# Which engine copies the K and V projections out of PSUM: from ScalarE to VectorE

## The chip, the cores and the metric

The kernel runs on the 8 cores of one Trainium2 chip. Each core works on its own part of the tokens with all the weights, and no core waits for another. The metric is the device time of the slowest core in microseconds (us).

## The reference

The reference is one transformer layer over x of shape (4, 2048, 2048), with a LayerNorm ahead of and behind each half:

```python
x = x + _layernorm(attn(_layernorm(x), Wq, Wk, Wv, Wo))
x = x + _layernorm(ffn(_layernorm(x), w_gate_up, w_down))
# attn: q = h @ Wq.T (16 heads), k = h @ Wk.T, v = h @ Wv.T (4 heads of 128)
#   softmax over a causal window of 1024 keys and 4 sink keys, then y @ Wo.T
# ffn: silu(h @ Wg.T) * (h @ Wu.T), then @ w_down.T; inner size 8192
```

Each core computes 1024 rows of the output. For the keys and values it needs up to 2048 token rows (`x_kv`).

## The kernel before, in words

The kernel is written in stages: (1) LayerNorm of the 2048 token rows, transposed to feature-major `h1f`, with the K and V projections in between; (2) the Q projection; (3) attention; (4) the output projection with residual and second LayerNorm; (5) the feed-forward part; (6) the last LayerNorm and the output. The change touches stage 1 alone.

Nothing schedules the work. A recorder (`Em`) takes tasks in the order in which the Python code emits them, and gives each engine its own queue in that order. It puts a semaphore wait ahead of a task where something that the task reads or overwrites is made or read on another engine (`task`, L43 to L97). So an engine that stands at a wait holds up everything behind it in its queue, whether that needs the awaited thing or not.

Stage 1 is a loop over 16 token tiles of 128 rows (L345 to L387); `idx` counts them from 0 to 15. Two buffers `xt` take turns for the tiles. For each tile the loop emits, in this order:

- the projections that have become possible. At idx 6 five V projections (`vproj`, L319 to L332), and from idx 7 on one in each tile, always for a tile whose `h1f` was made before. At idx 4, 8 and 12 also four K projections (`kproj`, L304 to L317). One projection is 16 matmuls of 512 columns into one PSUM bank, and one copy of that bank, cast to bf16, to SBUF (`kf` or `vt`). Six banks take turns (`bank512`).
- the load of the tile by a DMA from the POOL queue (L362), and (in the first tiles) the loading and casting of the weights of K and V.
- the statistics on VectorE: four BN_STATS (L275) and a BN_AGGR (L280), then on ScalarE a logarithm (L283) and an exponential (L286) that give `rstd`, and on VectorE one small operation for `nmr` (L290).
- the normalised tile `h1t` on ScalarE (L370), 16 transposes on TensorE (L378), and one copy of 2048 columns back to `h1f` on ScalarE (L385).

After the loop two more V projections and the last four K projections follow. Then the Q projection starts (L402): its weights are loaded by SP into two staging buffers `wst` and cast to bf16 `wqr` by ScalarE (L249), two casts for each of the first two heads ahead of the first matmul group.

Of the kernel before, what the change touches and what calls it, by code (L numbers as in the profile page):

```python
# [122 lines left out]
def build_nc():  # L123
# [91 lines left out]
    em = Em()  # L215
# [81 lines left out]
    def bank512():  # L297
        i = rot[0] % 6
        rot[0] += 1
        if i < 4:  # L300
            return PA[i], PAK[i]
        return PB[i - 4], PBK[i - 4]

    def kproj(m, ts):  # L304
        bk, bkk = bank512()
        fns = []
        for c in range(16):
            fns.append(lambda t, m=m, ts=ts, c=c, bk=bk: t.matmul(  # L308
                bk, wkbf.ap()[:, m * 2048 + c * 128:m * 2048 + (c + 1) * 128],
                h1f.ap()[:, c * 2048 + ts * 512:c * 2048 + (ts + 1) * 512],  # L310
                start=(c == 0), stop=(c == 15), skip_group_check=True))
        rd = [f"wk{m}"] + [f"h1_{4 * ts + i}_{g}" for i in range(4) for g in range(2)]
        em.task("tensor", fns, reads=rd, writes=[bkk])
        em.task("scalar",
                [lambda q, m=m, ts=ts, bk=bk: q.copy(
                    kf.ap()[:, m * 2048 + ts * 512:m * 2048 + (ts + 1) * 512], bk)],
                reads=[bkk], writes=[f"k_{m}_{ts}"])  # L317

    def vproj(tb):  # L319
        bk, bkk = bank512()  # L320
        fns = []
        for c in range(16):
            fns.append(lambda t, tb=tb, c=c, bk=bk: t.matmul(  # L323
                bk, h1f.ap()[:, c * 2048 + tb * 128:c * 2048 + (tb + 1) * 128],
                wvbf.ap()[:, c * 512:(c + 1) * 512],
                start=(c == 0), stop=(c == 15), skip_group_check=True))
        rd = [f"wv{c}" for c in range(16)] + [f"h1_{tb}_{g}" for g in range(2)]
        em.task("tensor", fns, reads=rd, writes=[bkk])
        em.task("scalar",
                [lambda q, tb=tb, bk=bk: q.copy(  # L330
                    vt.ap()[:, tb * 512:(tb + 1) * 512], bk)],
                reads=[bkk], writes=[f"v_{tb}"])  # L332

# [11 lines left out]
    for idx, tb in enumerate(TB_ORDER):  # L345
# [3 lines left out]
        if idx >= 6:  # L349
            while len(vback) > 1:  # L350
                vproj(vback.pop(0))
        if idx == 4:
            for m in range(4):
                kproj(m, 2)
        elif idx == 8:
            for m in range(4):
                kproj(m, 3)
        elif idx == 12:
            for m in range(4):
                kproj(m, 0)  # L360
# [28 lines left out]
    while vback:  # L389
        vproj(vback.pop(0))  # L390
# [5 lines left out]
    for me in range(16):  # L396
        r = me % 4
        for ts in range(2):
            bk, bkk = bank512()
# [541 lines left out]
```

How the kernel before makes its waits and increments, by code:

```python
    def replay(self, eng_obj, eng_name, sems):  # L108
        for waits, fns, inc in self.items[eng_name]:
            for (s, v) in waits:
                eng_obj.wait_ge(sems[s], 16 * v if s in self.streams else v)
            last = None
            for fn in fns:
                last = fn(eng_obj)
            if inc is not None and last is not None:
                last.then_inc(sems[inc[0]], inc[1])
```

## Time and profile before

| | us |
|---|---|
| median of 3 runs | 2387.99 (2293.54 to 2585.29) |
| the profiled execution | 2291.22 |
| its span, slowest core (core 7) | 2289.6 |
| spans of the 8 cores | 2283.2 to 2289.6 |
| stage 1 (start to the last K projection) | 254 |
| stage 2 (Q projection) | 113 |

The span is the time from the first to the last instruction of the slowest core; 1.6 us of the execution's time lie around it. The busy time of an engine is what the profiler records for its instructions.
### The profile page before, as it was taken

Reading aid. Unit: us, or ns where it says so; the run is one execution under the profiler, and the core shown is the slowest. Engines: PE = TensorE matmul, PEld = TensorE weight load, DVE = VectorE, ACT = ScalarE, POOL = GpSimd, SP = SyncE. Lnnn points to the kernel's source line nnn. Section 1 sums busy time; section 2 is a strip of 40 time slices with the busy share of each in tenths; the row PEclk is TensorE's granted clock in tenths of the full one; section 3 lists DMA queues with packets and bytes.
Section 4 is the critical chain, followed back from the end, with each engine's and each line's share of the span. In section 5 each row is a group of like instructions: output and inputs, shape, how many; then the busy total and the mean of one; then the engine's idle time right before and its main releaser. Section 6 shows DMA issues by size and latency. Waiting matters only on the chain.

```text
span 2289.6 us, 23911 instructions; the slowest of 8 cores (2283.2 to 2289.6 us)
## 1 busy us (share of the span) xinstructions
PE 2045.8 (89%) x9424; PEld 905.1 (40%) x9424; DVE 447.6 (20%) x592; ACT 918.9 (40%) x907; POOL 66.4 (3%) x87
## 2 busy tenths in 40 slices
PE   0776998998888886999999999999999999999983
PEld 0333443332223443444444444444444444444442
DVE  2122002543332541000121000110100110001135
ACT  4344344776663344333332333323333323333312
POOL 1100002400000000000000000000000000000000
PEclk9888999999999998999999999999999999999995
DMA  6321356501000333444553444643444634445526
GB/s 190 125 87 60 92 149 183 176 1 49 1 1 19 127 131 129 148 151 155 180 176 101 154 150 147 186 145 127 151 156 153 178 119 147 156 156 161 181 84 236
DMA packets 75566, 298.67 MB, mean 130 GB/s; under 512 B 8512, under 2 KB 8640, under 8 KB 69056
## 3 DMA queue, kind: packets, MB, share of 16 engines
q1 hardware_dynamic: 70848, 263.58, 36.8%
q0 software_dynamic: 4608, 33.56, 4.2%
q8 instruction: 77, 1.26, 0.2%
q14 instruction: 33, 0.27, 0.0%
HBM read 280.33 MB, written 16.78 MB: 130 GB/s over the span
## 4 chain that ended last, share of the span: by engine, by line
PE 84%; ACT 9%; DVE 2%; issue 2%; DMA 2%; ACTq 0%; DVEq 0%; SPq 0%; POOL 0%; POOLq 0%
PE ps_b L666 19%; PE ps_a L674 19%; PE ps_a L707 10%; PE ps_b L707 10%; ACT pt L451 5%; PE ps_a L442 5%; PE ps_a L402 3%; PE ps_a L582 3%; PE ps_b L500 2%; PE ps_b L491 2%; PE ps_a L308 2%; PE ps_a L323 2%; PE ps_b L582 2%; PE ps_b L402 2%; ACT h1t L370 1%
## 5 line engine op out<-in xcount | busy, mean ns | idle before, releaser
L249 ACT CAST wbf<-wst 128x1024 bf16<-128x1024 f32 x384 | 394.2, 1044 | 504.6 <-DMA wst<-wgu_pe 268.7
L666 PE MATMUL ps_b<-h2f,wbf 128*128 128x512 bf16 x2048 | 454.7, 380 | 4.0 <-ACT wbf L249 4.0
L674 PE MATMUL ps_a<-h2f,wbf 128*128 128x512 bf16 x2048 | 452.5, 379 | 0.0
L666 PEld LDWEIGHTS ps_b<-h2f,wbf 128*128 128x128 bf16 x2048 | 200.7, 98 | 247.6 <-issue 7.3
L674 PEld LDWEIGHTS ps_a<-h2f,wbf 128*128 128x128 bf16 x2048 | 200.6, 98 | 241.5
L686 DVE TENSOR_TENSOR a_sb<-silu_t,ps_a 128x1024 bf16<-128x1024 f32 x64 | 78.2, 1221 | 817.6 <-PE ps_a L674 741.7
L451 ACT ACTIVATE pt<-ps_a 128x2048 bf16<-128x2048 f32 x112 | 189.7, 1694 | 104.1 <-PE ps_a L442 100.3
L707 PE MATMUL ps_a<-a_sb,wbf 128*128 128x512 bf16 x1024 | 226.2, 379 | 5.9 <-DVE a_sb L686 5.9
L707 PE MATMUL ps_b<-a_sb,wbf 128*128 128x512 bf16 x1024 | 226.2, 379 | 0.0
L682 ACT ACTIVATE silu_t<-ps_b 128x1024 f32<-128x1024 f32 x64 | 65.5, 1024 | 347.1 <-PE ps_b L666 347.1
L469 DVE TENSOR_TENSOR pt<-pt,msk 128x2048 bf16<-128x2048 bf16 (+1 forms) x112 | 113.2, 1012 | 351.1 <-ACT pt L451 339.8
L707 PEld LDWEIGHTS ps_a<-a_sb,wbf 128*128 128x128 bf16 x1024 | 99.9, 98 | 127.7 <-issue 7.8
L707 PEld LDWEIGHTS ps_b<-a_sb,wbf 128*128 128x128 bf16 x1024 | 100.2, 98 | 120.8
L442 PE MATMUL ps_a<-qf,kf 128*128 128x512 bf16 x400 | 106.8, 385 | 45.3 <-ACT pt L451 44.4
L378 PE MATMUL ps_b<-i,h1t 128*128 128x128 bf16 x256 | 24.1, 269 | 100.5 <-ACT h1t L370 100.5
L491 PE MATMUL ps_b<-pt,vt 128*128 128x512 bf16 x400 | 107.2, 386 | 3.3 <-DVE yf L531 2.6
L500 PE MATMUL ps_b<-pt,ones_bf 128*1 128x512 bf16 x400 | 106.0, 383 | 0.0
L402 PE MATMUL ps_a<-h1f,wqr 128*128 128x512 bf16 x352 | 76.9, 379 | 2.7 <-ACT wqr L249 2.7
L442 PEld LDWEIGHTS ps_a<-qf,kf 128*128 128x128 bf16 x400 | 32.0, 97 | 118.2 <-issue 96.0
L582 PE MATMUL ps_a<-wo_bf,yf 128*128 128x512 bf16 x256 | 60.5, 400 | 6.3 <-ACT h2f L628 6.3
L378 PEld LDWEIGHTS ps_b<-i,h1t 128*128 128x128 bf16 x256 | 20.8, 122 | 106.6 <-issue 106.6
L582 PE MATMUL ps_b<-wo_bf,yf 128*128 128x512 bf16 x256 | 55.9, 379 | 6.3 <-ACT h2f L628 6.3
(103 smaller groups left out, 1082.5 us busy)
## 6 DMA issues: line engine op xcount, KB each, us to landing
wst<-wgu_pe SPq DMA_DIRECT2D x256, 512.0 KB, 4.2
wst<-wd_pe SPq DMA_DIRECT2D x128, 512.0 KB, 4.5
xt<-x_kv POOLq DMA_DIRECT2D x16, 1024.0 KB, 6.1
wst<-wq_pe SPq DMA_DIRECT2D x32, 512.0 KB, 4.4
wst<-wo_t SPq DMA_DIRECT2D x32, 512.0 KB, 4.4
xo<-x_kv POOLq DMA_DIRECT2D x8, 1024.0 KB, 7.1
wst<-wk_pe SPq DMA_DIRECT2D x8, 512.0 KB, 4.7
wst<-wv_t SPq DMA_DIRECT2D x16, 256.0 KB, 3.7
```

What stands on the lines that cost most here:

```text
L249: fn = [lambda g, d=dst_ap, sl=slot, n=n: g.copy(d, sl.ap()[:, 0:n])]
L402: fns.append(lambda t, r=r, ts=ts, c=c, bk=bk: t.matmul(bk, wqr[r].ap()[:, c * 128:(c + 1) * 128], h1f.ap()[:, c * 2048 + 1024 + ts * 512: ...
L442: t.matmul(dst, kf.ap()[:, kv * 2048 + kb * 128:kv * 2048 + (kb + 1) * 128], qf.ap()[:, hh * 1024 + qs * 512:hh * 1024 + (qs + 1) * 512], ...
L451: [lambda q, src=pa[:, 0:512 * ln], st0=st0, ln=ln: q.activation(pt.ap()[:, st0 * 512:(st0 + ln) * 512], src, AF.Exp, scale=SCALE)],
L469: [lambda v, a=a, b=b: v.tensor_tensor(pt.ap()[:, a * 512:(a + b) * 512], pt.ap()[:, a * 512:(a + b) * 512], msk.ap()[:, a * 512:(a + b) * ...
L491: t.matmul(yb, vt.ap()[:, kb * 512 + kv * 128:kb * 512 + (kv + 1) * 128], pt.ap()[:, s_ * 512:(s_ + 1) * 512], start=first, stop=last, ski ...
L500: t.matmul(zb[0:1, :], ones_bf.ap(), pt.ap()[:, s_ * 512:(s_ + 1) * 512], start=first, stop=last, skip_group_check=True))
L582: fns.append(lambda t, c=c, ms=ms, tb=tb, bk=banks[ms][0]: t.matmul(bk, yf.ap()[:, c * 1024 + tb * 128:c * 1024 + (tb + 1) * 128], wo_bf.a ...
L666: fns.append(lambda t, c=c, ts=ts, rg=rg: t.matmul(PB[ts], wbf[rg].ap()[:, c * 128:(c + 1) * 128], h2f.ap()[:, c * 1024 + ts * 512:c * 102 ...
L674: fns.append(lambda t, c=c, ts=ts, ru=ru: t.matmul(pa[:, ts * 512:(ts + 1) * 512], wbf[ru].ap()[:, c * 128:(c + 1) * 128], h2f.ap()[:, c * ...
L686: [lambda v, jj=jj: v.tensor_tensor(a_sb.ap()[:, jj * 1024:(jj + 1) * 1024], silu_t.ap(), pa[:, 0:1024], ALU.mult)],
L707: fns.append(lambda t, ic=ic, ts=ts, r=r, dps=dps: t.matmul(dps[ts], wbf[r].ap()[:, ic * 128:(ic + 1) * 128], a_sb.ap()[:, ic * 1024 + ts ...
```

## The change

The copy out of PSUM at the end of each K and V projection goes to VectorE instead of ScalarE. Buffers, sizes, matmuls, DMAs and the place in the code stay. These are 16 copies to `kf` and 16 to `vt`, 32 in all.

```diff
@@ kproj, L314
-        em.task("scalar",
-                [lambda q, m=m, ts=ts, bk=bk: q.copy(
+        em.task("vector",
+                [lambda v, m=m, ts=ts, bk=bk: v.tensor_copy(
                     kf.ap()[:, m * 2048 + ts * 512:m * 2048 + (ts + 1) * 512], bk)],
                 reads=[bkk], writes=[f"k_{m}_{ts}"])
@@ vproj, L329
-        em.task("scalar",
-                [lambda q, tb=tb, bk=bk: q.copy(
+        em.task("vector",
+                [lambda v, tb=tb, bk=bk: v.tensor_copy(
                     vt.ap()[:, tb * 512:(tb + 1) * 512], bk)],
                 reads=[bkk], writes=[f"v_{tb}"])
```

Since each engine keeps the order in which the code emits, the copies move from ScalarE's queue to the same point of the emission in VectorE's queue. The orders of TensorE, POOL and SP stay as they are.

VectorE's queue before, over two tiles of the middle of the loop. In all of these rows `xt_48` and `xt_49` are the two token buffers, `bn_84` and `bn_85` the statistics of the first, `bn6b` and `bn2b` those of the second.

```order
L290 TENSOR_SCALAR nmrb<-bn2b,rstdb 128x1
L275 BN_STATS bn_84<-xt_48 128x6 x4
L280 BN_AGGR bn_85<-bn_84 128x2
L290 TENSOR_SCALAR nmr<-bn_85,rstd 128x1
L275 BN_STATS bn6b<-xt_49 128x6 x4
L280 BN_AGGR bn2b<-bn6b 128x2
L290 TENSOR_SCALAR nmrb<-bn2b,rstdb 128x1
```

The same place with the change (tiles 9 and 10):

```order
L290 TENSOR_SCALAR nmr<-bn_85,rstd 128x1
L330 CAST vt<-ps_a 128x512
L275 BN_STATS bn6b<-xt_49 128x6 x4
L280 BN_AGGR bn2b<-bn6b 128x2
L290 TENSOR_SCALAR nmrb<-bn2b,rstdb 128x1
L330 CAST vt<-ps_b 128x512
L275 BN_STATS bn_84<-xt_48 128x6 x4
L280 BN_AGGR bn_85<-bn_84 128x2
L290 TENSOR_SCALAR nmr<-bn_85,rstd 128x1
```

A copy to `vt` now stands between `nmr` of one tile and the statistics of the next. At tiles 4, 8 and 12 copies to `kf` stand there too.

ScalarE's queue before, from tile 15 to the start of the Q projection:

```order
L370 ACTIVATE h1t_51<-xt_49,nmrb,rstdb 128x2048
L385 COPY h1f<-ps_b 128x16x128
L330 CAST vt<-ps_a 128x512 x2
L315 CAST kf<-ps_b 128x512 x2
L315 CAST kf<-ps_a 128x512 x2
L249 CAST wqr_52<-wst_77 128x1024
L249 CAST wqr_52<-wst_78 128x1024
```

The same place with the change:

```order
L283 ACTIVATE rstdb<-bn2b,eps_sb 128x1
L286 ACTIVATE rstdb<-rstdb 128x1
L370 ACTIVATE h1t_51<-xt_49,nmrb,rstdb 128x2048
L385 COPY h1f<-ps_b 128x16x128
L249 CAST wqr_52<-wst_77 128x1024
L249 CAST wqr_52<-wst_78 128x1024
```

The casts of the first Q weights now stand directly behind the last copy to `h1f`, ahead of where the last six copies were.

## Rows read from the trace of the kernel before

**Rows 1.** The page: span, and busy time of each engine with its share.
```profile
span 2289.6 us, 23911 instructions; the slowest of 8 cores (2283.2 to 2289.6 us)
PE 2045.8 (89%) x9424; PEld 905.1 (40%) x9424; DVE 447.6 (20%) x592; ACT 918.9 (40%) x907; POOL 66.4 (3%) x87
```

**Rows 2.** Busy time by stretch: from:to, length, then the columns as named.
```profile
core 7: us, PE busy (x) PEld busy (x) DVE busy (x) ACT busy (x) POOL busy (x), PEclk, DMA share, GB/s
111.00:254.00 143.00, 105.00 (x528) 49.73 (x528) 25.93 (x55) 56.95 (x63) 4.22 (x8) 0.89 0.17 59
```

**Rows 3.** Waits from 111 to 254 us: total us, times, longest.
```profile
PE ps_b L378 <- ACT h1t L370: 38.2, 10, 3.8
```

**Rows 4.** Chain of waits, one tile and more: start us, us, what.
```profile
155.25 0.30 ACT rstdb L283
...
156.25 2.10 ACT h1t L370
...
158.49 1.05 PE ps_b L378 x16
159.54 3.47 PE ps_b L323 x16
```

**Rows 5.** Timeline of ScalarE and VectorE: start, us, engine, what, [idle before].
```profile
154.76 0.59 ACT L330 CAST vt<-ps_a 128x512 bf16<-128x512 f32 x1 [3.27 <-PE ps_a L323]
156.07 2.46 DVE L275 BATCH_NORM_STATS2 bn<-xt 128x6 f32<-128x512 f32 x4
```

**Rows 6.** Chain of waits at tile 3, where the statistics ended last.
```profile
52.86 2.48 DVE bn6b L275 x4
...
55.79 0.30 ACT rstdb L283
```

**Rows 7.** Groups on VectorE, whole span: xcount | busy, mean ns | idle before.
```profile
L715 DVE COPY out_fm<-ps_a 128x512 f32<-128x512 f32 x8 | 5.5, 692 | 46.6 <-PE ps_a L707 46.6
L469 DVE TENSOR_TENSOR pt<-pt,msk 128x512 bf16<-128x512 bf16 x32 | 13.6, 425 | 23.5 <-ACT pt L451 23.5
L275 DVE BATCH_NORM_STATS2 bn<-xt 128x6 f32<-128x512 f32 x32 | 19.7, 680 | 21.6 <-DMA xt<-x_kv 21.6
```

**Rows 8.** Timeline: the last copy to h1f, and the first Q matmuls.
```profile
231.69 1.87 ACT L385 COPY h1f<-ps_b 128x2048 bf16<-128x2048 bf16 x1 [1.29 <-PE ps_b L378]
...
256.72 5.56 PE L402 MATMUL ps_a<-h1f,wqr 128*128 128x512 bf16 x25 [2.71 <-ACT wqr L249]
```

**Rows 9.** Groups from 111 to 254 us: transposes, and statistics of one buffer.
```profile
L378 PE MATMUL ps_b<-i,h1t 128*128 128x128 bf16 x160 | 12.9, 245 | 38.2 <-ACT h1t L370 38.2
...
L275 DVE BATCH_NORM_STATS2 bn<-xt 128x6 f32<-128x512 f32 x16 | 9.9, 679 | 0.0
```

**Rows 10.** Chain of waits: matmuls behind idle times, transposes (L378) and projections.
```profile
115.71 5.14 PE ps_a L323 x16
...
166.81 1.87 PE ps_b L378 x16
168.68 4.26 PE ps_b L323 x16
...
182.92 10.36 PE ps_a L308 x48
...
221.69 5.06 PE ps_a L323 x16
```

**Rows 11.** Busy time by stretch, columns as in rows 2.
```profile
90.00:95.00 5.00, 4.91 (x24) 2.87 (x25) 2.67 (x5) 1.87 (x1) 0.53 (x1) 0.50 0.49 175
95.20:110.90 15.70, 15.62 (x73) 6.84 (x71) 0.00 (x0) 2.34 (x4) 0.00 (x0) 1.00 0.02 6
```

**Rows 12.** Timeline of TensorE: transposes, and weight loads at the lower clock.
```profile
90.09 1.86 PE L378 MATMUL ps_b<-i,h1t 128*128 128x128 bf16 x16 [5.10 <-ACT h1t L370]
...
115.93 0.15 PEld L323 LDWEIGHTS ps_a<-wvbf,h1f 128*128 128x128 bf16 x1 [0.28 <-issue]
...
118.49 0.15 PEld L323 LDWEIGHTS ps_a<-wvbf,h1f 128*128 128x128 bf16 x1 [0.28 <-issue]
```

## The prediction

> **What bounds the kernel now.** I read the page first. TensorE is busy for 89% of the span and ScalarE and VectorE for 40% and 20% [rows 1], so as a whole this is a kernel of TensorE, and an edit on the other two counts only where TensorE stands waiting for them. The second view is the busy time by stretch. From 111 to 254 us, the main part of stage 1, TensorE is busy for 105.0 of 143 us, while ScalarE has 57.0 and VectorE 25.9 us of work [rows 2]. No engine is full there, so the stage is bound by a loop of waits and not by an engine. The third view, the waits of that stretch, names it: TensorE stands ten times, 3.8 us each, 38.2 us in all, at the transposes, for `h1t` from ScalarE [rows 3]. Those are all its waits of note.
>
> The fourth view, the chain of waits, shows the loop itself [rows 4]. A V projection ends, its copy on ScalarE takes the chain until the logarithm (start at 155.25), then come the exponential, `nmr`, 2.10 us of `h1t`, the transposes, and the next V projection. The reader should note what is absent: the four BN_STATS. VectorE runs them at 156.07, right behind `nmr` of the tile before, beside `h1t` (156.25) [rows 4, 5], and has nothing but an aggregate until the next `nmr`. The statistics are free today because nothing stands ahead of them in VectorE's queue.
>
> **The change part by part.** In the timeline a copy on ScalarE starts at 154.76 [rows 5] and the logarithm behind it at 155.25 [rows 4]: the copy's price in the chain is 0.49 us. It is removed. The logarithm needs only the statistics, and could start early if these were early. They aren't. In VectorE's new queue the copy to `vt` stands between `nmr` and the statistics of the next tile, and this copy waits for the V projection that TensorE runs behind the transposes. So the statistics can't start before the projection's end. The new chain from there is: copy, statistics, logarithm.
>
> The copy from PSUM on VectorE isn't in this trace with bf16 output. The nearest row is the copy of 128x512 f32 out of the same PSUM, 692 ns, and the other side is an operation on 512 columns of bf16, 425 ns [rows 7]. I take 0.69, the row that reads PSUM. From the start of the statistics to the start of the logarithm it is 55.79 - 52.86 = 2.93 us; tile 3 shows it, where they ended last [rows 6]. Together 0.69 + 2.93 - 0.49 = 3.13 us more in each pass.
>
> How many passes? The queue has copies ahead of the statistics at tile 4 (K), tile 6 (five V) and tiles 7 to 15: 11 tiles. At tile 5 nothing stands between, and the first four tiles are as before. 11 x 3.13 = **34.4 us**. The V projections that stand together, and the four K projections in a row, add nothing more: a projection at the full clock takes 10.36 / 3 = 3.45 us [rows 10], far above 0.69, and only the last copy of a row is followed by statistics. Bounds: with 0.43 for the copy it is 11 x 2.87 = 31.6 us.
>
> The end of the stage gains. Before, the casts of the first Q weights stood behind the last copy to `kf`, and TensorE waited 2.71 us for them [rows 8]. Now they stand behind the last `h1f` copy, which ends at 231.69 + 1.87 = 233.6, over 20 us ahead of 256.72 [rows 8], beside two V and four K projections. **-2.7 us**, between 0 (should the wait be for something else) and 2.7.
>
> Third, the clock. TensorE's idle time per tile grows from 3.82 to 3.82 + 3.13 = 6.95 us. Transposes took 1.05 us at the full clock [rows 4] and 1.87 at the lower level, at 166.81 [rows 10]. In the ten tiles from 111 us on they took 12.9 us [rows 9]. If all ten run at the lower level, as they did at 90.09 after 5.10 us of idle time [rows 12], that is 18.7: **+5.8 us**. The V projections behind them took between 3.47 and 5.15 us, ten in all, with the sum 47.3 (115.71 and 221.69 are the first and the last but one) [rows 10]. They hold lower-clock time already. After transposes at the lower level I find 4.26 us in one tile [rows 10], and at 90 us the lower level lasts until 95 and then the engine has 1.00 [rows 11], which makes about 5.1 us for the projection. The middle, 4.7, is what the mean is now, so I put this at 0. Bounds: 10 x 4.26 is 4.7 us less than 47.3. At the lower level a matmul follows the last every (118.49 - 115.93) / 6 = 0.427 us [rows 12], so ten projections wholly at it take 68.3 us, 21.0 more.
>
> The page "TensorE: Matmul & The Clock Gate" of the Trainium skill (Part 1) says that the throttled state is the default and that activity releases it, with two levels only. The trace agrees in the levels, 0.50 and 1.00. By that rule alone a loop with more idle time can end anywhere between 0 and +21.0; it is the base of the first rival.
>
> What else moves is hidden. PSUM banks come free 0.2 us later at most, and six take turns. The loads of `xt` wait for `h1t`, not for the copies. VectorE's extra work, 32 x 0.69 = 22 us, lies in its idle time. The attention reads `kf` and `vt` more than 100 us later.
>
> The sum: 34.4 - 2.7 + 5.8 = +37.5 us. The profiled execution took 2291.22 us (2289.6 of span [rows 1] and 1.6 around it), so the forecast is **2329 us**, 1.6% more. The median of the three runs shown, 2387.99, lies 4.2% above that execution and the lowest, 2293.54, beside it; my sum speaks of an execution like the profiled one.
>
> **The rivals.** *The lower clock stays through the V projections.* This is the case on the slower side. Place: the ten V projections behind transposes. TensorE would work about 8.7 of 15.6 us per tile where it now works 6 of 10, and if that no longer brings the full clock, the cost is the 21.0 us above: 37.5 + 21.0 = +58.5, 2350 us. It decides (over 2%, 45.8 us) once these projections take a mean of 4.73 + 0.83 = 5.56 us. For it: the idle time nearly doubles. Against it: at 90 us the engine had stood for 5.10 us [rows 12] and yet was at 1.00 by 95.2 [rows 11].
>
> *ScalarE set free pays.* With the copy gone, the logarithm could run while TensorE is at the V projection, and `h1t` would be ready when the projection ends. The 3.82 us of idle time at 11 tiles go and the 2.7 at the end: -44.7, 2246 us. The order of VectorE's queue speaks against it: the statistics stand behind the copy, so the logarithm's input isn't there. For it only the shares speak, 57.0 against 25.9 us. The Trainium skill's page "TensorEngine Tiling (Array Packing)", PSUM Bottleneck, says to "Use both ScalarE and VectorE for PSUM evacuation"; by that rule the time would be this one. No stretch here shows either engine as the limit.
>
> *The statistics waited anyway.* If the token load ended last in each tile, statistics behind a copy would cost only 0.69 - 0.49: 11 x 0.2 - 2.7, about 2291 us. VectorE does wait for `xt`, 21.6 us in all for one buffer [rows 7], but from 111 us on, over 16 of its BN_STATS, 0.0 [rows 9].
>
> **How the numbers follow.** Forecast 0.74; lower clock throughout 0.19; ScalarE set free 0.03; statistics waited anyway 0.04. About 2% is what a measurement of this kernel can tell from no change. The forecast and the last case are within it, so same is 0.78, slower 0.19, faster 0.03. The forecast's own range is 37.5 - 2.8 - 4.7 = +30.0 to 37.5 + 4 + 2.7 = +44.2 (projections at 5.1 us, nothing won at the end): 2321 to 2335. Executions differ by 0.3% (the spans of the cores in rows 1), which takes the low end to 2315. The high end has to take in 2350, and also that the time measured is a median like that of before: 2388 plus the sum is 2426. So 2315 to 2426.
>
> **What would show it.** In the profile after, the chain of waits should hold, in 11 tiles, the copy on VectorE, four BN_STATS of some 2.5 us and the aggregate ahead of the logarithm. The wait of the transposes for `h1t` should be near 7.0 us instead of 3.8. Transposes should take 1.87 us in all ten tiles, the V projections 4.3 to 5.1. The last K projection should end near 254 + 40 = 294 us, and the first Q matmul follow without a wait; from there on all is as before, shifted. I am wrong if the statistics start before the copy, if the wait is still 3.8 us, or if the stretch from 111 us on grows by under 20 or over 60 us.

## The result, and the profile after

| | before | with the change |
|---|---|---|
| median, us | 2293.6 (10 runs) | 2330.98 (9 runs) |
| lowest, us | 2290.12 | 2329.16 |
| profiled execution: span of the slowest core | 2289.6 | 2328.9 |

The ratio of the two is 1.0168, with a 95% interval of 1.0155 to 1.018: the changed kernel is slower by 1.7%. Four of the ten times before (two of the three behind the median of 2387.99 among them) and two of the nine after come from executions that the machine had disturbed; without these the medians are 2292.03 and 2330.42 us, 38.4 us apart, and every comparison and median below leaves such times out.

The page of the kernel after, its span and busy times, as in [rows 1]:

```profile
span 2328.9 us, 23738 instructions; the slowest of 8 cores (2320.8 to 2328.9 us)
PE 2036.9 (87%) x9241; PEld 910.2 (39%) x9424; DVE 466.6 (20%) x624; ACT 901.5 (39%) x875; POOL 67.2 (3%) x87
```

VectorE has 32 instructions and 19 us more, ScalarE 32 and 17 us less. These sums say nothing about the 38 us. The waits of the stretch from 111 us to the end of stage 1, the view of [rows 3], do (total us, times, longest):

```profile
ACT rstd L283 <- DVE bn L280: 74.2, 5, 20.4
...
PE ps_b L378 <- ACT h1t L370: 68.8, 10, 6.9
...
ACT rstdb L283 <- DVE bn2b L280: 32.6, 5, 6.6
```

TensorE's ten waits for `h1t` have grown from 38.2 us to 68.8, from 3.8 to 6.9 us each. And two rows are new: ScalarE's logarithm (L283) now waits for the aggregate of the statistics (L280), which before was always there in time. The chain of waits after, one tile (start us, us, what), beside [rows 4]:

```profile
129.88 0.06 DVE vt L330
129.94 0.55 issue
130.49 2.48 DVE bn6b L275 x4
133.06 0.28 DVE bn2b L280
...
133.42 0.30 ACT rstdb L283
...
134.42 2.10 ACT h1t L370
136.52 0.14 issue
136.66 1.86 PE ps_b L378 x16
138.52 4.86 PE ps_b L323 x16
```

The copy starts at 129.88, the statistics at 130.49, the logarithm at 133.42: 3.54 us from the copy's start, where it was 0.49 before (154.76 to 155.25 in [rows 4, 5]). The four BN_STATS have come onto the path as a whole. In the chain of the whole stage they stand there, directly behind a copy, in 11 tiles: 4 and 6 to 15.

The groups of the same stretch, transposes and the copies to `vt` (busy us, mean ns | idle before):

```profile
L378 PE MATMUL ps_b<-i,h1t 128*128 128x128 bf16 x160 | 18.6, 308 | 68.8 <-ACT h1t L370 68.8
...
L330 DVE CAST vt<-ps_a 128x512 bf16<-128x512 f32 x9 | 6.2, 691 | 63.3 <-PE ps_a L323 63.3
```

The transposes of ten tiles took 12.9 us before [rows 9] and take 18.6 now, 1.86 each: all at the lower clock. The copy on VectorE takes 691 ns. And the timeline at the end of the stage, beside [rows 8]:

```profile
276.81 1.99 ACT L249 CAST wqr<-wst 128x1024 bf16<-128x1024 f32 x2
...
290.06 7.07 PE L308 MATMUL ps_a<-h1f,wkbf 128*128 128x512 bf16 x31
...
296.97 7.07 PE L402 MATMUL ps_a<-h1f,wqr 128*128 128x512 bf16 x31
```

The first Q weights are cast 20 us ahead of need, and the Q projection follows the last K projection without the 2.71 us of idle time.

The sum over these rows: 11 tiles x 3.06 us more idle time (6.88 against 3.82 in each) = +33.7; transposes 18.6 - 12.9 = +5.7; the ten V projections behind transposes took 48.7 us in the chain against 47.3, +1.4; the end -2.7. That is +38.1 us, against 38.4 between the medians.

### The profile page after: what moved, and what is told of

It reads as the page before. It is cut to its first block, busy times and chain, and to the rows that moved or that the text cites. A ratio compares the mean times of both kernels' runs of the same rounds, so it can differ in the third digit from the quotient of the medians.

```text
span 2328.9 us, 23738 instructions; the slowest of 8 cores (2320.8 to 2328.9 us)
## 1 busy us (share of the span) xinstructions
PE 2036.9 (87%) x9241; PEld 910.2 (39%) x9424; DVE 466.6 (20%) x624; ACT 901.5 (39%) x875; POOL 67.2 (3%) x87
## 4 chain that ended last, share of the span: by engine, by line
PE 82%; ACT 9%; DVE 4%; issue 3%; DMA 2%; ACTq 0%; DVEq 0%; SPq 0%; POOL 0%; POOLq 0%
PE ps_b L666 19%; PE ps_a L674 19%; PE ps_a L707 9%; PE ps_b L707 9%; ACT pt L451 5%; PE ps_a L442 4%; PE ps_a L402 3%; PE ps_a L582 2%; PE ps_b L500 2%; PE ps_b L491 2%; PE ps_a L308 2%; PE ps_a L323 2%; PE ps_b L582 2%; PE ps_b L402 1%; ACT h1t L370 1%
## 5 line engine op out<-in xcount | busy, mean ns | idle before, releaser
L378 PE MATMUL ps_b<-i,h1t 128*128 128x128 bf16 x256 | 29.8, 308 | 137.1 <-ACT h1t L370 137.1
L442 PE MATMUL ps_a<-qf,kf 128*128 128x512 bf16 x386 | 105.0, 386 | 47.1 <-ACT pt L451 45.5
L378 PEld LDWEIGHTS ps_b<-i,h1t 128*128 128x128 bf16 x256 | 26.0, 142 | 143.1 <-issue 143.1
```

The source lines that it names most:

```text
L442: t.matmul(dst, kf.ap()[:, kv * 2048 + kb * 128:kv * 2048 + (kb + 1) * 128], qf.ap()[:, hh * 1024 + qs * 512:hh * 1024 + (qs + 1) * 512], ...
```

## The experiments

The theory was that the cost is a matter of place in VectorE's in-order queue: what stands behind a copy waits for TensorE. The main rival was that the copies themselves cost, each its share, or that VectorE is a bad engine for them.

**One kind of copy at a time.** Two kernels, the first with only the hunk in `kproj` of the diff, the second with only the hunk in `vproj`:

```diff
 # k only: kproj as in the changed kernel; v only: vproj as in the changed kernel
-        em.task("scalar",
-                [lambda q, m=m, ts=ts, bk=bk: q.copy(
+        em.task("vector",
+                [lambda v, m=m, ts=ts, bk=bk: v.tensor_copy(
```

> Only the 16 copies to kf go to VectorE, the 16 to vt stay on ScalarE. Theory (the cost is the place in VectorE's queue: each tile whose statistics stand behind a copy pays 3.06 us): only tiles 4, 8 and 12 pay, 3 x 3.06 = 9.2 us, about 1 us of clock for two sets of transposes, and the first Q casts stand behind two vt copies only, -2.6 us. Together +7.6 us: 2300 us against 2292. Rival (each moved copy costs its share, whatever stands behind it): half of the 38 us, 2311 us.

> Only the 16 copies to vt go to VectorE. Theory (place in the queue): tiles 6, 7, 9, 10, 11, 13, 14 and 15 pay, 8 x 3.06 = 24.5 us; at tiles 8 and 12 the statistics run while TensorE is at the K projections and cost nothing; the Q casts still stand behind the kf copies on ScalarE, so the wait of 2.7 us stays. With some 4 to 6 us of clock: +30, 2322 us. Rival (each moved copy costs its share): 2311 us.

Measured: the copies to `kf` alone 1.0037 (1.0024 to 1.005), +8.5 us on 2290; the copies to `vt` alone 1.0136 (1.0116 to 1.0156), +31 us, from two times, 2321.7 and 2322.02. Both move 16 copies, so a price per copy would have made them equal. With the 2.6 us that the first kernel wins at the first Q casts added back they are 11.1 and 31, or 3.7 and 3.9 us for each of 3 and 8 tiles, clock included. With the copies to `vt` alone, VectorE's timeline at tile 8 and behind it shows why 8 and not 10:

```profile
141.50 0.26 DVE L280 BATCH_NORM_AGGREGATE bn<-bn 128x2 f32<-128x24 f32 x1
153.31 0.21 DVE L290 TENSOR_SCALAR nmr<-bn,rstd 128x1 f32<-128x1 f32 x1 [11.54 <-ACT rstd L286]
162.15 0.69 DVE L330 CAST vt<-ps_a 128x512 bf16<-128x512 f32 x1 [8.63 <-PE ps_a L323]
162.76 2.46 DVE L275 BATCH_NORM_STATS2 bn6b<-xt 128x6 f32<-128x512 f32 x4
```

At 153.31 `nmr` is preceded by 11.54 us of idle time: the statistics of that tile had been done by 141.76, while TensorE was still at four K projections. In the next tile they start at 162.76, directly behind the copy that waited for TensorE, and their 2.46 us are on the path.

**The statistics, doubled.** If they are on the path only after the change, doing them twice costs after and not before.

```diff
+        em.task("vector",
+                [lambda v, j=j, s=s, b6=STT[par][0]: v.bn_stats(
+                    b6.ap()[:, 6 * j:6 * j + 6], xt[s].ap()[:, 512 * j:512 * (j + 1)])
+                 for j in range(4)],
+                reads=[f"xt{s}"], writes=["bn6" + sx])
         ln_stats([(xt[s].ap(), 2048)], [f"xt{s}"], 4, par, emit_nmr=True)
```

> The kernel after with the four BN_STATS of each tile in stage 1 done twice (the same result). Theory (the statistics are on the path in 11 tiles): each extra set costs 2.46 us in 11 tiles and in tile 3, some 29 us: 2360 us. Rival (the loss comes from the copy itself or its wait, the statistics are hidden as before): no more than 5 us, 2336 us.

> The kernel before with the four BN_STATS of each tile in stage 1 done twice. Theory (the statistics are hidden before, save in tile 3 where they wait for the token load): +2.5 us, 2295 us. Rival (they are on the path before too): +27 us or more, 2320 us.

Measured on the kernel before: 1.0002 (0.9977 to 1.0026), no change that can be told from none. The medians, 2291.79 and 2289.06, are 2.7 us apart; 2.5 were expected, from tile 3. On the kernel after: 1.0332 (1.0304 to 1.036) against before. That rests on two times, 2359.79 and 2371.46, and is too high, because in the second time cores 0 and 1 took at least 10 us more than cores 3 to 7. The lower time is 30.6 above the lowest of the changed kernel. Cores 4 to 7 of the profiled execution took 2351.6 to 2355.4 us, where those of the changed kernel took 2324.9 to 2326.6: 28.6 us between the medians, and 29 were expected. The chain of waits holds both sets:

```profile
119.81 2.47 DVE bn L369 x4
...
122.37 2.48 DVE bn L275 x4
...
124.95 0.28 DVE bn L280
...
125.31 0.30 ACT rstd L283
```

**The order instead of the engine.** If only the place counts, the copies may stay on VectorE once the statistics stand ahead of them. The block that emits the projections of a tile was moved down: to position A with the copies on either engine, and to position B with the copies on ScalarE. The diff is shortened, and its two comments mark where the block went.

```diff
-        if idx >= 6:
-            ...
-                kproj(m, 0)
         em.task("gpsimd", ...)          # load of the tile
         ln_stats([(xt[s].ap(), 2048)], [f"xt{s}"], 4, par, emit_nmr=True)
+        # position A: projections here (statistics, rstd, nmr first)
         em.task("scalar", ...)          # h1t
+        # position B: projections here (h1t first as well)
```

> The kernel after, with load, statistics, rstd and nmr of a tile emitted ahead of its projections, so that they stand ahead of the copies in VectorE's queue; nothing else changed. Theory (place in the queue): the cost goes and ScalarE, free of copies, makes h1t beside the projection; a tile takes some 6.3 us instead of 13.6 (before: near 9.8), the wait of the transposes falls under 2 us, and the kernel beats both: about 2247 us. Rival (copies out of PSUM are simply worse on VectorE, or VectorE's work in the stage is the limit): it stays above before, 2300 us or more.

> The kernel before (copies on ScalarE), with load, statistics and also h1t of a tile emitted ahead of its projections. Theory (the order alone decides, the engine of the copy hardly): h1t is made beside the projection here too, and only the 2.7 us at the first Q casts stay: about 2250 us, within 5 us of the run with statistics first. Rival (taking the copies off ScalarE is what makes that run fast): this one stays near 2280 us or above.

> The kernel before (copies on ScalarE), with load, statistics, rstd and nmr ahead of the projections, but h1t behind them. Theory (what must not stand behind a copy is every step of the normalisation): h1t still stands behind the copy on ScalarE, and only logarithm, exponential and nmr, 1.0 us, leave the path of 11 tiles: about 2280 us. With the copies on VectorE the same order gave 2247. Rival (the statistics alone matter): no change against before, 2290 us, since they were hidden there; or 2247, if the order of the statistics is all.

> The run with statistics first and copies on VectorE once more, in more rounds, on one chip with the next. Three of its five times were near 2245 to 2247 us and one at 2266. Theory (order alone): 2246 us, within 5 us of the next run. Rival (the engine of the copy matters as well): it is over 10 us ahead of the next run.

> The run with the normalised tile first and copies on ScalarE once more. One of its four times was 2245 us and three 2263 to 2268, so its median is unclear. Theory (order alone): 2246 to 2250 us. Rival (the copies on ScalarE cost 15 to 20 us even so): 2264 us.

| copies on | projections | ratio to before | 95% interval | median, us |
|---|---|---|---|---|
| VectorE | position A | 0.9825 | 0.9783 to 0.9867 | 2246.01 |
| VectorE | position A, again | 0.9815 | 0.9802 to 0.9829 | 2249.25 |
| ScalarE | position B | 0.9867 | 0.9824 to 0.991 | 2263.76 |
| ScalarE | position B, again | 0.9812 | 0.9798 to 0.9825 | 2247.88 |
| ScalarE | position A | 0.9909 | 0.9894 to 0.9924 | 2270.08 |

With the order put right, the same 32 copies on VectorE make a kernel that is 1.9% faster than before and 3.5% faster than the changed one. The copies on ScalarE do as well one position further down: in the repetition the two medians are 1.4 us apart. The first set of position B had three of four times near 2265, and the first set of position A with the copies on VectorE had one. In these four times some of the cores took 2256 to 2267 us and the rest 2232 to 2245, as in the repetition. So the order of the code does not make them; what does is open.

Position A on ScalarE is the run that separates the steps. There `h1t` still stands behind the copy. The theory said -11 us, it was -21: right in sign and place, too small in size. The waits from 111 us on:

```profile
PE ps_b L378 <- ACT h1t L370: 28.1, 10, 2.8
```

The idle time per tile fell from 3.8 to 2.8 us, the 1.0 us that was expected, 11 us in all. The rest is the clock: the transposes fell to 1.05 us each, 10.5 in all against 12.9, and of the ten V projections seven took 3.5 us and three about 5.1, where before nine took 4.3 to 5.15. That is 2.4 and about 7.6 us, 10 together.

With the same position A the copies on VectorE are 21 to 24 us ahead of the copies on ScalarE. So the engine of the copy is not without effect: what counts is whether `h1t`, or the statistics, stand behind a copy in its queue. Position B with the copies on VectorE was not run. With the copies on VectorE in position A, and on ScalarE in position B, `h1t` overlaps the projection, as the same view shows for these two in turn:

```profile
PE ps_b L378 <- ACT h1t L370: 14.4, 7, 2.8
```

```profile
PE ps_b L378 <- ACT h1t L358: 12.4, 7, 2.3
```

**The first Q weights, cast early, by themselves.** `stage_wq(0)` was emitted ahead of the last two V and four K projections in the kernel before.

```diff
+    stage_wq(0)
     while vback:
         vproj(vback.pop(0))
     for m in range(4):
         kproj(m, 1)
-
-    stage_wq(0)
```

> The kernel before with the two casts of the first Q weights emitted ahead of the last two V and four K projections, so ahead of the last six copies in ScalarE's queue. Theory (the change wins the wait of the first Q matmul): -2.6 us, 2289.5 us, and no wait ahead of the first Q matmul. Rival (that wait has another cause, such as the transfer): no change.

Measured: 0.999 (0.9981 to 1.0), medians 2287.33 and 2289.06, so -1.7 us, or -2.3 by the ratio; -2.6 was expected, and the interval touches 1. The timeline shows the wait gone: the Q projection's matmuls carry no idle time ahead of them.

```profile
249.72 3.19 PE L308 MATMUL ps_a<-h1f,wkbf 128*128 128x512 bf16 x14
252.75 7.07 PE L402 MATMUL ps_a<-h1f,wqr 128*128 128x512 bf16 x32
```

**The idle time filled, to price the clock.** Matmuls whose result nobody reads were put behind the projections of tiles 4 and 6 to 15, 28 in the changed kernel and 15 in the kernel before. They are extra work, but 28 of them take 6.05 us and 15 take 3.24, and so they fit into the idle times of 6.88 and 3.82 us.

```diff
+        if idx == 4 or idx >= 6:
+            di = rot[0] % 6              # the next PSUM bank, unused now
+            ...
+            em.task("tensor",
+                    [lambda t, c=c, dbk=dbk: t.matmul(
+                        dbk, wkbf.ap()[:, (c % 16) * 128:(c % 16 + 1) * 128],
+                        h1f.ap()[:, (c % 16) * 2048 + 1024:(c % 16) * 2048 + 1536],
+                        start=(c == 0), stop=(c == 28 - 1), skip_group_check=True)
+                     for c in range(28)], ...)
```

> The kernel after with 28 matmuls of 512 columns into the next, unused PSUM bank behind the projections of tiles 4 and 6 to 15; their result is overwritten. They fill TensorE's idle time of 6.9 us with 6.05 us at the full clock. Theory (a part of the loss, and of the time before, is the lower clock behind idle time): transposes take 1.05 us instead of 1.86 and V projections 3.47 instead of 4.8; 10 x 0.8 + 10 x 1.35 = -22 us, 2309 us. Rival (the clock costs nothing, or the extra matmuls outlast the idle time): 2331 us or more.

> The kernel before with 15 matmuls of 512 columns (3.24 us at the full clock) into the unused PSUM bank behind the projections of tiles 4 and 6 to 15, into TensorE's idle time of 3.8 us. Theory (the clock falls for idle time here too, though less): transposes -2.4 us, V projections 47.3 to 34.7, -12.6, together -15: 2275 us. Rival (idle time of 3.8 us costs no clock): 2290 us or more.

Measured: the changed kernel with 28 extra matmuls per tile has a median of 2306.03 us, 24 us less than without them, or 22 by the ratios (1.0071, 1.0057 to 1.0086, against before); 22 were expected. The kernel before with 15 has 2276.9, 0.9937 (0.9923 to 0.995), -14.5 us, where -15 was expected. The groups of the two in turn, transposes and V projections:

```profile
L323 PE MATMUL ps_a<-wvbf,h1f 128*128 128x512 bf16 x133 | 29.8, 379 | 0.0
...
L389 PE MATMUL ps_b<-i,h1t 128*128 128x128 bf16 x160 | 10.5, 219 | 8.4 <-ACT h1t L381 8.4
```

```profile
L323 PE MATMUL ps_a<-wvbf,h1f 128*128 128x512 bf16 x135 | 30.9, 379 | 0.4
...
L389 PE MATMUL ps_b<-i,h1t 128*128 128x128 bf16 x160 | 10.5, 219 | 5.8 <-ACT h1t L381 5.8
```

In both, every group reads as at the full clock, 219 ns for a transpose and 379 for a matmul, and the transposes wait less for `h1t` only because the idle time is filled. Against the kernel before, as measured beside each, the two are at +17.0 (2306.03 - 2289.06) and -14.5 us (2276.9 - 2291.37), 31.4 apart, or 30.7 by the ratios. That is the change's price in waits alone, near 33.7 - 2.7 = 31.0; the other 7 to 8 of the 38.4 us are the clock, where the rows gave 5.7 + 1.4 = 7.1.

## Where the prediction held, and the step that failed

The prediction gave 2329 us, +37.5 on the profiled execution. Measured are 2330.98 us, +38.4 between the medians and +39.2 between the two profiled executions. The mechanism and the terms of the sum held; the step from the sum to a forecast did not.

*The step that failed* is the base. The sum was added to the profiled execution, 2291.22, while the time before stood in the table as 2387.99. Against that, 2329 is a fall of 2.5%, and the kernel became slower by 1.7%. For the high end the text took the other base: "the time measured is a median like that of before: 2388 plus the sum is 2426". That median was no property of the kernel: 2292.03 is, from times between 2290.12 and 2293.66. The lowest of the three times shown, 2293.54, beside the profiled 2291.22, was the sign of which base to take for both. The range from the costs alone, 2321 to 2335, holds the result, and what was put on top of it, up to 2426, was not needed.

*What a measurement can tell* was mis-sized too. "About 2% is what a measurement of this kernel can tell from no change" has no row behind it, and it put a forecast of 1.6% more under the word same, with 0.78. The interval of the ratio is 1.0155 to 1.018: a rise of 1.7% is clear of no change by more than ten times the interval's half width. The 0.3% given for executions was read from the cores of one execution; the times behind the medians spread over 0.15% before and 0.1% after.

*The main term.* "0.69 + 2.93 - 0.49 = 3.13 us more in each pass" was 3.06: the copy's 0.69 overlaps the statistics by 0.08 (129.88 to 130.49 is 0.61). The place was right: the doubled statistics cost 2.7 us before and about 29 after. So was the count of 11 passes, which the chain shows and the split by kind of copy bears out, 3 for `kf` and 8 for `vt`.

*The end of the stage.* "-2.7 us" is confirmed by the row without idle time; done alone it gave about -2, at the edge of what could be told. The last K projection was to end near 294 and ended at 297.0. In that execution the first K projection started at 65.87 instead of 63.00, and over the cores of either profiled execution this start lies between 60.0 and 65.9, so the 3 us lie within what cores differ by and are not put down to the change.

*The clock.* "+5.8 us" for the transposes was 5.7. The V projections, put at 0, cost 1.4: they took 4.8 to 4.9 us each, all alike, in place of 3.5 to 5.15. The 0 came from the middle between two readings, 4.26 and 5.1, and that the true mean lay so near was in part luck. The two filled runs put the clock's part of the change at 7 to 8 us.

*The rivals.* The lower clock throughout did not come: the V projections took 4.8 to 4.9 us each, where 6.83 was worked out for it. "ScalarE set free pays" did not come for the reason given, the order in VectorE's queue. The experiment that puts the order right gives the number that this rival had worked out, 2246 us there, 2246.01 and 2249.25 measured, but not by its sum. It had 42.0 us of idle time going and no clock. In the repetition TensorE's waits for `h1t` from 80 us to the end of the stage fell from 47.1 to 20.6 us, 26.5 less; the transposes took 3.2 us less, and the V projections 59.5 us for the 248 matmuls that the trace holds instead of 71.8 for 256. That the two sums meet is luck. The statistics did not wait anyway.

*A miss behind the prediction* was position A on ScalarE, -21 us instead of -11: the expectation left out the clock, which gave back 10 us with 1.0 us less idle time per tile.

## What to carry to other kernels

Before moving work to the less busy engine, look at what stands behind it in that engine's queue. A copy that waits for TensorE turns everything behind it into part of the path, even work that was free before; here the order of emission was worth 42 us, and the best kernels with the copies on either engine were 1.4 us apart. In other orders the engine did matter, since it decides what stands behind the copy: in the old order VectorE was 38 us behind ScalarE, at position A 21 or more ahead. And where TensorE stops for a few microseconds in each round of a loop, count its clock as well as the wait. Before a forecast is given, take one base for the sum, the range and the comparison, and look at the single times behind a median.

## What the runs showed of the hardware

Where TensorE stood idle for 3.82 us in each tile, the lower clock behind that cost the kernel before 15 us (2291.4 to 2276.9 with the idle time filled). With 2.8 us per tile, at position A with the copies on ScalarE, all ten sets of transposes took 1.05 us. The length of the idle time alone doesn't decide it, though: before, five of the ten sets took 1.05 to 1.07 us and one 1.87, all ten behind 3.82 us, and at position A with the copies on VectorE one set took 1.86 us behind 2.79. Extra matmuls that nobody reads made a kernel faster, by 15 and by 24 us.

A copy of 128x512 f32 from PSUM to bf16 takes 691 ns on VectorE and 586 on ScalarE [rows 5], and the next instruction starts 0.61 and 0.49 us after it. In 11 passes that difference is 1.3 us.
